# Feed-forward of an attention and FP4 block on one core: codes turned four to a word, block scales spread by DMA, rests on GpSimd

## What is computed

```
def fp4_quant_dequant(x):            # blocks of 16 along the last dim
    scale = max(max|xb| / 6, 1e-12)
    q = GRID[searchsorted(MID, |xb / scale|)] * sign(xb) * scale   # GRID 0, .5, 1, 1.5, 2, 3, 4, 6
x = x + attention(layernorm(x))      # ends with attn @ W_O
y = fp4(layernorm(x))
h = silu(y @ fp4(w_gate).T) * (y @ fp4(w_up).T)      # 512 -> 1408
x = x + fp4(h) @ fp4(w_down).T                       # 1408 -> 512
```

## Time and profile before

| what | value |
|---|---|
| median of three runs | 3055.09 us |
| span of the profiled execution | 3055.2 us (the page gives no other time for it) |
| PE busy | 2987.2 us, 98% of the span |
| DVE busy | 2625.3 us, 86% |
| ACT busy | 1349.6 us, 44% |
| POOL busy | 753.2 us, 25% |
| one tile of the feed-forward (WO of one tile to WO of the next) | 27.04 us |

### The profile page before, as it was taken

One profiled execution on the slowest core, in us unless ns is written; L12 is line 12 of the kernel. 1 busy time (PEld: TensorE's weight loads), 2 busy tenths in 40 slices (PEclk: granted clock), 3 DMA queues, 4 the chain that ended last, 5 costly groups with the idle time before them and its releaser, 6 DMA issues.

```text
span 3055.2 us, 65829 instructions
## 1 busy us (share of the span) xinstructions
PE 2987.2 (98%) x23204; PEld 2207.4 (72%) x23204; DVE 2625.3 (86%) x4209; ACT 1349.6 (44%) x2010; POOL 753.2 (25%) x680
## 2 busy tenths in 40 slices
PE   7999899999999999889999999999999999999999
PEld 6787644444444444478888888888888888888887
DVE  7999788888888889788888888888888888888886
ACT  5666577777777777632222222222222222222221
POOL 2444200000000000023333333333333333333332
PEclk9999999999999999999999999999999999999999
DMA  7889956666656656521111111111111111111110
GB/s 244 284 289 300 274 121 144 135 140 143 138 140 140 141 139 138 151 86 37 42 42 42 42 33 36 42 41 42 35 38 37 42 42 41 39 30 41 42 35 14
DMA packets 251214, 304.22 MB, mean 100 GB/s; under 512 B 25553, under 2 KB 158545, under 8 KB 251089
## 3 DMA queue, kind: packets, MB, share of 16 engines
q1 hardware_dynamic: 251088, 302.89, 36.7%
HBM read 190.35 MB, written 112.46 MB: 99 GB/s over the span
## 4 chain that ended last, share of the span: by engine, by line
PE 56%; DVE 1%; ACT 0%; DMA 0%; issue 0%; POOL 0%; SPq 0%; DVEq 0%
PE p_ring L1847 20%; PE p_ring L1875 15%; PE ps_od L1847 11%; PE ps_od L1827 5%; PE p_ring L1865 2%; PE p_ring L1855 1%; DVE sb_wg_lo L1753 0%; PE ps_od L1875 0%; PE p_ring L1827 0%; PE p_ring L1890 0%; DVE sb_fp_tmp L102 0%; DVE sb_wd_lo L1753 0%; DMA dn<-sb_fp_tmp 0%; DVE sb_h_amax L88 0%; DVE sb_stage L1724 0%
## 5 line engine op out<-in xcount | busy, mean ns | idle before, releaser
L1042 ACT ACTIVATE sb_probs<-scores 128x1024 f32<-128x1024 f32 (+3 forms) x512 | 405.7, 839 | 118.9 <-PE scores L1248 112.7
L790 POOL TENSOR_TENSOR sb_at_in<-sb_at_in,sb_inv_in 128x512 f32<-128x512 f32 x64 | 85.7, 1339 | 1080.4 <-DMA sb_inv_in<-dinv 1079.6
L1847 PE MATMUL p_ring<-sb_wg_hi,sb_xq_hi 128*128 128x512 f32 (+1 forms) x1024 | 294.8, 369 | 0.3 <-DVE sb_wd_lo L1753 0.3
L1550 POOL TENSOR_TENSOR sb_stage<-sb_stage,sb_h_inv 128x512 f32<-128x512 f32 (+1 forms) x192 | 210.3, 1095 | 340.0 <-DVE sb_h_inv L94 340.0
L1847 PE MATMUL p_ring<-sb_wg_lo,sb_xq_hi 128*128 128x512 f32 (+1 forms) x1024 | 290.9, 365 | 0.0
L1847 PE MATMUL p_ring<-sb_wg_hi,sb_xq_lo 128*128 128x512 f32 (+1 forms) x1024 | 289.9, 364 | 0.0
L1248 PEld LDWEIGHTS scores<-sb_q_hi,sb_k_hi 32*128 32x128 f32 x1536 | 73.8, 182 | 285.5 <-ACT sb_probs L1042 155.3
L1875 PE MATMUL p_ring<-sb_wd_hi,sb_ht_hi 128*128 128x512 f32 x693 | 275.9, 398 | 0.0
L1875 PE MATMUL p_ring<-sb_wd_hi,sb_ht_lo 128*128 128x512 f32 x693 | 270.2, 390 | 0.0
L1875 PE MATMUL p_ring<-sb_wd_lo,sb_ht_hi 128*128 128x512 f32 x693 | 269.8, 389 | 0.0
L1556 POOL TENSOR_TENSOR sb_stage<-sb_stage,sb_h_scale 128x512 f32<-128x512 f32 (+1 forms) x192 | 189.8, 988 | 267.8 <-DVE sb_stage L104 267.8
(11 more groups left out here) (203 smaller groups left out, 7170.4 us busy)
## 6 DMA issues: line engine op xcount, KB each, us to landing
kq<-sb_kq_out SPq DMA_DIRECT2D x32, 1024.0 KB, 7.3
sb_kq_raw<-kq SPq DMA_DIRECT2D x64, 512.0 KB, 10.0
sb_xin<-in_L_attn_x_dram SPq DMA_DIRECT2D x32, 512.0 KB, 6.9
v<-sb_v_out SPq DMA_DIRECT2D x64, 256.0 KB, 6.5
rq<-sb_r_out SPq DMA_DIRECT2D x64, 256.0 KB, 4.4
sb_qr<-rq SPq DMA_DIRECT2D x256, 64.0 KB
sb_kr_hi<-kr SPq DMA_DIRECT2D x32, 512.0 KB
sb_kr_lo<-kr SPq DMA_DIRECT2D x32, 512.0 KB
```

The lines of the kernel that those rows point to most:

```text
L1042: act.activation(probs(k)[:, 2 * pair:2 * pair + 2, off:BANK], scores[(2 * k + pair) % RING2][:, :, off:BANK], ACT.Exp, scale=SCALE).then_ ...
L1550: pool.tensor_tensor(x, x, spread(h_inv[:, a // QB:b // QB], (b - a) // QB), ALU.mult).then_inc(h_y, 1)
L1847: i = pe.matmul(ps[:, m, 0:b0 - a0], xt[a][:, c, :], wg[b][:, m, c, a0:b0], start=(c == 0 and a == b == 0), stop=(c == DC - 1 and a == 1))
```

## The change

The hidden values and x are no longer multiplied by their scales before they are turned. The rounding runs at a scale that makes the rounded value a small multiple of 2^-23, and ScalarE turns it into an unsigned byte around 64 (`code_x`, `code_hidden`). Four bytes are one 32-bit word, so that one transpose of 128x128 words turns 512 features. TensorE does 1 transpose for x (was 4), 2 in HT0 (was 8) and 1 in HT1 (was 3).

The block scales are turned in 32x32 blocks by a VectorE transpose (one for x, three for the hidden slices), stored by a DMA into a small tensor in HBM, and loaded from it again by a DMA that repeats each scale over the partitions of its block. VectorE then reads the bytes from PSUM, subtracts 64 and multiplies by the spread scales (`decode`). ScalarE rounds the product from SBUF, and GpSimd forms the rest from SBUF (`rest_of_x`, `rest_of_hidden`), where VectorE did it from PSUM. GpSimd's `hidden_q` is gone. Silu is written into the place of the hidden values. x is loaded straight into `x1` by a DMA of its own (`load_x`). Down and gate wait for GpSimd's rests (`ht_rest`, `x_rest`) in place of VectorE's.

```
-X_STEPS = 1 + SCALES_STEPS + 1 + ROUND_STEPS + 1
+X_STEPS = 1 + SCALES_STEPS + 1 + ROUND_STEPS
...
# SyncE, per tile (new): for x and for each slice s
+            def spread_h_scale(q, r, s):
+                sp.wait_ge(h_turned_done, count(q, r, 3, s + 1))
+                sp.dma_start(by_blocks(h_sc[s]), h_turned[:, s]).then_inc(h_scale_stored, 16)
+                sp.wait_ge(h_scale_stored, count(q, r, 48, 16 * s + 16))
+                if s < 2:
+                    sp.dma_start(h_spread[s], h_sc[s].unsqueeze(1).to_broadcast([P // CODES, CODES, P])
+                                 ).then_inc(h_spread_loaded[0], 16)
+                else:
+                    for c in range(3):
...
# SyncE body
                 if exists(q, r + 3):
                     sp.wait_ge(ahead.at_divided, count(q, r, 1, 3))
                     ahead.load_inverse(sp, b, j + 3)
+                if exists(q, r + 1):
+                    store_x_scale(q, r + 1)
+                    spread_x_scale(q, r + 1)
+                for s in range(3):
+                    spread_h_scale(q, r, s)
+                if exists(q, r - 1):
+                    store(b, j - 1)
...
# GpSimd
-            def hidden_q(q, r, s):
...
+            def rest_of_x(q, r):
+                pool.wait_ge(x_hi, count(q, r, 1, 1))
+                pool.tensor_tensor(xt_lo[:], x_values, xt_hi[:].bitcast(F32), ALU.subtract).then_inc(x_rest, 1)
+            def rest_of_hidden(q, r, j):
+                a, b = HT_CHUNKS[j]
+                pool.wait_ge(ht_rounded, count(q, r, 2, j + 1))
+                pool.tensor_tensor(ht_lo[:, a:b], values(j), ht_hi[:, a:b].bitcast(F32), ALU.subtract).then_inc(ht_rest, 1)
...
# ScalarE
+            def code_x(q, r):
+                act.wait_ge(x_chain, count(q, r, X_STEPS, X_STEPS))
+                act.activation(x_codes[:].bitcast(U8), xq[:], ACT.Identity, bias=code_zero[:],
+                               scale=CODE_STEP).then_inc(x_coded, 1)
             def round_hidden(q, r, j):
-                act.wait_ge(ps_ready, number(q, r, name) + 1)
-                act.copy(ht_hi[:, a:b], src[:, 0:b - a]).then_inc(ht_rounded, 1)
+                act.wait_ge(ps_free, number(q, r, f"HT{j}") + RING3 + 1)
+                act.copy(ht_hi[:, a:b], values(j)).then_inc(ht_rounded, 1)
...
                 if exists(q, r - 1):
                     round_hidden(q, r, 1)
+                if exists(q, r + 1) and not first:
+                    code_x(q, r + 1)
...
                 silu_of(q, r, 1)
                 magic_h(q, r, 0)
...
# VectorE
+            def decode(out, words, scales):
+                return dve.scalar_tensor_tensor(out=out, in0=bytes_of(words)[:, 0:out.shape[1]],
+                                                scalar=CODE_ZERO, in1=scales, op0=ALU.subtract, op1=ALU.mult)
-            def rest_of_hidden(q, r, j):
-                dve.wait_ge(ht_rounded, count(q, r - 1, 2, j + 1))
...
+            def decode_hidden(q, r, j):
+                dve.wait_ge(h_spread_loaded[j], count(q, r - 1, (32, 48)[j], (32, 48)[j]))
+                ps = read_out(q, r, f"HT{j}")
...
# TensorE
             def down(q, r):
                 ps = start(q, r + 1, "DN")
-                pe.wait_ge(ps_free, number(q, r + 1, "HT1") + RING3 + 1)
+                pe.wait_ge(ht_rest, count(q, r, 2, 2))
```

More of the change, by code:

```diff
@@ L21 @@
 I32 = mybir.dt.int32
+U8 = mybir.dt.uint8
 ALU = mybir.AluOpType
@@ L744, in __init__ @@
         self.in_loaded = [sem(f"in_loaded{i}") for i in range(2)]
+        self.x_loaded = [sem(f"ffn_x_loaded{i}") for i in range(2)]
         self.loads = [sem(f"prep_loaded{i}") for i in range(PREP_SLOTS + LATE_SLOTS)]
@@ L1000, in _ @@
         def _(pool):
-            ahead.divide_tile(pool, 0, 16 * NI, 32)
+            ahead.divide_tile(pool, 0, 16 * NI, 16)
         @block.scalar
@@ L1386, in feed_forward @@
         h_round = sem("h_round")
-        h_q = sem("h_q")
+        h_coded = sem("h_coded")
         ht_rounded = sem("ht_rounded")
+        ht_rest = sem("ht_rest")
+        constants = sem("ffn_constants")
+        x_coded = sem("x_coded")
+        x_rest = sem("x_rest")
+        x_turned_done = sem("x_scale_turned")
+        x_scale_stored = sem("x_scale_stored")
+        x_spread_loaded = sem("x_spread_loaded")
+        h_turned_done = sem("h_scale_turned")
+        h_scale_stored = sem("h_scale_stored")
+        h_spread_loaded = [sem(f"h_spread_loaded{j}") for j in range(2)]
         stored = [sem(f"out_stored{i}") for i in range(4)]
@@ L1430, in iterations, with bytes_of, values @@
             four(bodies - 1)
+        def bytes_of(words):
+            return words.bitcast(U8).rearrange("p (q c) -> p c q", c=CODES)
+        def values(j):
+            return (h_values[:], rest_q)[j]
         def h_slot(r, s):
@@ L1490, in _ @@
             ahead.load_chunk(sp, 2 * B - 1)
+            ahead.load_x(sp, 0, 1)
             ahead.load_tile(sp, 0, 2)
@@ L1496, in body @@
                 q, r = b * HALF + j // UNROLL3, j % UNROLL3
+                if exists(q, r + 2):
+                    sp.wait_ge(stored[(r + 2) % 4], count(q, (r + 2) // 4 * 4, 4, 16))
+                    ahead.load_x(sp, b, j + 2)
                 if exists(q, r + 3):
@@ L1535, in divide @@
             def divide(q, r):
-                ahead.divide_tile(pool, r % 2, count(q, r, 16 * NI, 16 * NI), count(q, r // 2 * 2, 16, 32))
+                ahead.divide_tile(pool, r % 2, count(q, r, 16 * NI, 16 * NI), count(q, r // 2 * 2, 8, 16))
             def rest_of_attention(q, r):
@@ L1569, in body @@
                     rest_of_attention(q, r + 2)
+                if exists(q, r - 1):
+                    rest_of_hidden(q, r - 1, 1)
                 hidden_y(q, r, 1)
-                hidden_q(q, r, 0)
                 hidden_y(q, r, 2)
-                hidden_q(q, r, 1)
-                hidden_q(q, r, 2)
+                if exists(q, r + 1):
+                    rest_of_x(q, r + 1)
             iterations(pool, body)
+            for j in range(2):
+                rest_of_hidden(bodies - 1, 3, j)
         @block.scalar
@@ L1889, in turn_weights @@
                 for c in range(w // P):
-                    i = pe.transpose(job_bank(n)[:, c * P:(c + 1) * P], slot(n)[:, c * P:(c + 1) * P], ident[:])
+                    features = slice(c, w, CODES) if w == D else slice(c * P, (c + 1) * P)
+                    i = pe.transpose(job_bank(n)[:, c * P:(c + 1) * P], slot(n)[:, features], ident[:])
                 i.then_inc(turned, 1)
```

186 lines of the change are left out of this document (124 added, 62 removed).

## The result

| | before | after |
|---|---|---|
| median of the runs, us | 3054.44 (3053.5 to 3056.8, four) | 3419.48 (3415.2 to 3424.3, four) |
| ratio, with its 95% interval | | 1.1189 (1.1176 to 1.1202) |
| profiled span, us | 3055.2 | 3422.6 |
| mean granted clock of TensorE | 0.995 | 0.944 |

A forecast was written before the change was run, and what follows sets the result against it. TensorE bounds the kernel at 27.04 us a tile; VectorE's chain of 25.6 - 0.1 + 1.6 + 3.2 = 30.3 us becomes the bound. 62 tiles give +202 us, the ends 2 and 7: 3266 us, range 3165 to 3345.

The forecast's parts named there:

- the third rival: In the tile, byte reads at 1.22 us or DN at TensorE's lower clock: 3330 to 3390 us; chance 0.14.
- Ahead of the first tile ... about 2 us: Before the first tile, the relay of x's scales and the new steps cost about 2 us.
- both ends: About 2 us ahead of the first tile; at the last tile +7, from the spread (5) and a GpSimd rest (2.5).
- VectorE's chain: VectorE's own time for a feed-forward tile after the change: 25.6 - 0.1 + 1.6 + 3.2 = 30.3 us.
- the base of 25.6: VectorE's own chain for a tile before the change: 27.04 - 1.41 = 25.6 us.
- Silu of slice 1, 1.6: At slice 1's product VectorE waits for silu, behind the cast of 384 and coding of x: 1.6 us a tile.
- GpSimd against VectorE, 3.2: GpSimd's rests hold up VectorE's steps in a tile: 1.8 + 1.0 + 1.15 - 0.69 = +3.3, taken as 3.2 us.
- the wide rest: GpSimd's rest of 1024, after HT0's decode, makes VectorE's scale step (line 90) wait 1.8 us.
- TensorE's 1.20 us a tile: 15 transposes become 4 on TensorE, so 1.20 us go, leaving 25.84 us a tile.
- the relay by DMA hidden: The scales' DMA store and load, about 5 us with waits, lie under about 7 us of VectorE work and waits.
- the signs named for "wrong": Tile under 27 us with TensorE at 98%, decodes above 1 us, granted clock below 0.9, or VectorE waiting for a DMA.
- Silu of slice 0 ... forced: VectorE's 1.18 us wait for silu at slice 0's product was called no spare time, passing whatever TensorE does.

The follow-up runs named there:

- the experiment: Load of x for tile 1 moved right behind that of tile 0, against the kernel with reordered ScalarE and GpSimd (3014.7 us): 3003.3 us, ratio 0.9828.
- the run with few transposes: Kernel before with 11 of the 15 transposes of a tile left out in tiles 4 to 63: 2990.5 us, ratio 0.9776.
- the filled kernel: Kernel after with 12 matmuls on data at hand put ahead of DN's wait: 3301.5 us, ratio 1.0797.
- once DN was early: Kernel after with GpSimd's rest of 384 ahead of the attention's rest: 3250.2 us; with silu of slice 1 also moved earlier on ScalarE: 3163.1 us.
- six fillers: Kernel after with 6 matmuls on data at hand put ahead of DN's wait: 3301.1 us, ratio 1.081.

## Why the prediction was wrong, and where it was right

- **The step that failed: the sum left DN at its old 7.52 us behind the idle time that the sum itself had found.** It had TensorE idle "some 4.4 us a tile, mostly ahead of DN", put the clock at nothing, and left the effect to the third rival, "More than summed", at 0.14. DN took 10.42 us, its first 12 matmuls at the lower clock. The rival named the very loop (GpSimd's rest, DN, WO, residual) and a price of "1 to 2 us"; measured 32.6 - 30.6 = 2.0 us a tile, 118 us in all. The price was not open, as the prediction has it: the trace of the kernel before has 3.66 us idle ahead of its first HT0, and the 1.8 us that HT0 and G0 lost behind it. An idle stretch in every tile was part of the forecast, so this price belonged in the sum: 30.3 + 1.8 would have been 32.1 us a tile, against 32.6 measured. The Trainium skill, TensorE: Matmul & The Clock Gate, section HAM oscillation — how this bites in real kernels, says that repeated waits ahead of short groups of matmuls put each group back to the low clock; the trace agrees, 0.43 us a matmul for 12 of 33 and 0.23 for the rest.
- **"Ahead of the first tile ... about 2 us": 11.7 in the phase.** The load of x for tile 1 was passed over; it is 6.7 of them, by the experiment. The other 5 are not told apart. The whole of both ends is 3419.5 - 3055 - 62 x (32.6 - 27.04) = 20 us, where 9 had been taken; 2.3 of it lie ahead of the phase.
- **VectorE's chain came out right:** 30.3 forecast, 30.2 read, and 30.6 a tile at full clock, 0.35 of that still a wait at the residual. That it fits to 0.1 us is in part luck, for the base of 25.6 it starts from was 25.0 in the run with few transposes. 3266 compares with the 3301 of the filled kernel: 0.3 x 62 = 19 us of tile, some 11 at the ends, and 5 not told apart.
- **Silu of slice 1, 1.6: measured 1.68**, for the coding takes 0.72. But its price on the time was nil in the kernel after and 87 us once DN was early: two loops of nearly one length share the tile, and each hides the other's cost.
- **GpSimd against VectorE, 3.2:** the wide rest gave 1.85 us a tile and 1.81 in the row. The Trainium skill, SBUF — State Buffer, section Who interferes with whom, lets tensor_scalar, the instruction of line 108, enter a mode in which it waits for a GpSimd instruction that came first; the row of line 108 agrees, 0.18 us alone and 1.99 under the rest. The other terms are in the rows and were not tried alone: the rest of x 1.55 - 0.56 = 0.99 (line 122 at 384 columns, against the same step of the kernel before; 1.0 summed), and at slice 1 line 108 0.94 and line 112 0.53 against 0.18 each, 1.11 (1.15 summed).
- **TensorE's 1.20 us a tile: 1.13**, and the relay by DMA hidden, as said. Of the signs named for "wrong", the granted clock came near its mark of 0.9: 0.92 in the middle of the feed-forward.
- **"Silu of slice 0 ... forced":** it was not; the edit that moves it, with GpSimd's division, gave 84 us.

## What to carry to other kernels

When a change leaves TensorE idle for some microseconds ahead of a group of matmuls in every pass, price that group at the lower clock over its first matmuls, and follow it to whoever waits for the group; a few dummy matmuls ahead of the wait test it, as 6 and 12 did here. When two loops are nearly equal, taking a wait out of one shows nothing until the other is shortened: try the edits together before one is called worthless. What is moved to engines with time to spare needs its place in their order chosen anew: the same instructions took 3419 us in one order and 3003 in another.

## What the runs showed of the hardware

- Idle of 3.4 us ahead of DN: clock 0.92 over 500 us; 2.6 us: 0.95; 2.0 us behind six fillers: 1.00. Waits of 0.4, 1.1 and 1.4 us in one tile, none ahead of DN: 1.00. These are four kernels, not a rule, and the busy time ahead of the idle stretch differs between them.
- A VectorE instruction of 32 columns, 0.18 us alone, took 1.99 us beside a GpSimd instruction of 2.40 us and ended 0.04 us behind it: its delay was what was left of the GpSimd instruction, ten times its own length.
- A decode that reads bytes from PSUM and floats from SBUF took 0.687 us for 512 columns, as much as one on floats; the coding on ScalarE took 0.72 us, against 0.63 for the multiplication by 2^22, which writes floats. The coding also adds a bias read from SBUF; which of the two costs the 0.09 us is not told apart.
